# Decoder block on one core: FFN rows split before they are transposed, low parts of the GELU on GpSimd, scores at the head of a slot, and no zero products in the last stage

## The reference

```python
x = x + attn(layernorm(x), Wq, Wk, Wv, Wo, Wa, Wb, conv taps)   # gated delta rule, 16 heads of 128, values 256 wide
x = x + xattn(layernorm(x), ctx, ctx)                           # 32 query heads of 8 on 8 key/value heads
x = x + ffn(layernorm(x), w1, b1, w2, b2)                       # 256 -> 1024 -> 256

# xattn, per sequence and head, 64 x 64 scores
scores = q @ k.T / sqrt(8); attn = softmax(scores); out = attn @ v
# ffn
w1q, w2q = ternary(w1), ternary(w2)                # -1, 0, 1
h = gelu(x @ w1q.T + b1)                           # exact form
y = h @ w2q.T + b2
```

## Time and profile before

| | us |
|---|---|
| Median of three runs (2300.52 to 2302.37) | 2301.5 |
| Profiled execution, own time | 2296.62 |
| Its span | 2294.8 |
| Mean granted TensorE clock | 0.993 |
| PE busy | 2099.4 (91%) |
| DVE busy | 1846.1 (80%) |
| ACT busy | 1534.8 (67%) |
| POOL busy | 967.0 (42%) |

### The profile page before, as it was taken

One profiled execution on the slowest core, in us unless ns is written; L12 is line 12 of the kernel. 1 busy time (PEld: TensorE's weight loads), 2 busy tenths in 40 slices (PEclk: granted clock), 3 DMA queues, 4 the chain that ended last, 5 costly groups with the idle time before them and its releaser, 6 DMA issues.

```text
span 2294.8 us, 61471 instructions
## 1 busy us (share of the span) xinstructions
PE 2099.4 (91%) x23576; PEld 1356.7 (59%) x23576; DVE 1846.1 (80%) x2942; ACT 1534.8 (67%) x2881; POOL 967.0 (42%) x1312
## 2 busy tenths in 40 slices
PE   2499799999999999999999999999888889999998
PEld 2244365665665665665565665665555667777776
DVE  6888788898888889889888988889766556666665
ACT  3498677777777777777777777777656345555554
POOL 1006756282653827446283553827450112222222
PEclk9999999999999999999999999999999989999999
DMA  8535433333233333324323333332321200111100
GB/s 288 191 132 189 137 88 97 85 95 99 67 101 95 84 96 90 94 78 108 94 76 91 85 101 84 94 95 73 101 59 42 61 16 28 34 34 33 34 17 20
DMA packets 360817, 199.97 MB, mean 87 GB/s; under 512 B 304336, under 2 KB 313296, under 8 KB 358608
## 3 DMA queue, kind: packets, MB, share of 16 engines
q1 hardware_dynamic: 360528, 196.04, 30.2%
HBM read 123.87 MB, written 72.09 MB: 85 GB/s over the span
## 4 chain that ended last, share of the span: by engine, by line
PE 72%; ACT 12%; issue 6%; DVE 5%; POOL 3%; DMA 2%; SPq 1%; ACTq 0%; DVEq 0%; POOLq 0%
PE PS L1304 22%; PE PS L1318 15%; PE PS L1382 6%; PE PS L1397 5%; ACT XN L785 4%; PE PS L1553 4%; PE PS L1355 3%; ACT Y L762 3%; PE PS L1482 3%; PE PS L1515 3%; PE PS L1543 2%; PE PS L1339 2%; PE PS L1501 2%; PE PS L1346 2%; PE PS L1529 1%
## 5 line engine op out<-in xcount | busy, mean ns | idle before, releaser
L1031 DVE SCALAR_TENSOR_TENSOR Y<-PS,CW,Y 128x504 f32<-128x504 f32 (+2 forms) x1536 | 1114.3, 732 | 231.8 <-ACT Y L755 198.2
L1304 PE MATMUL PS<-XT,WH 128*128 128x512 f16 x2048 | 614.6, 382 | 6.6 <-DVE Y L1031 6.6
L755 ACT ACTIVATE Y<-PS,CW 128x512 f32<-128x512 f32 x512 | 394.3, 773 | 320.6 <-PE PS L1304 316.1
L1304 PE MATMUL PS<-XT,WL 128*128 128x512 f16 x1024 | 388.8, 380 | 0.0
L1318 PE MATMUL PS<-WOS,XN 128*128 128x256 f16 x3072 | 377.7, 273 | 3.4 <-DVE XN L1046 2.3
L1318 PEld LDWEIGHTS PS<-WOS,XN 128*128 128x128 f16 x3072 | 300.6, 98 | 94.0 <-DVE XN L1046 4.0
L610 POOL TENSOR_TENSOR SCR<-SCR 128x31 f32<-128x31 f32 (+15 forms) x496 | 288.5, 582 | 38.9
L1304 PEld LDWEIGHTS PS<-XT,WH 128*128 128x128 f16 x2048 | 168.5, 98 | 208.1 <-issue 40.5
L607 POOL TENSOR_TENSOR SCR<-SCR 128x31 f32<-128x31 f32 (+15 forms) x496 | 269.7, 544 | 38.9
L585 POOL TENSOR_SCALAR KD<-SCR 128x32 f32<-128x32 f32 x16 | 5.4, 339 | 659.9 <-DMA SCR<-PGD 659.9
L785 ACT ACTIVATE XN<-PS,KN 128x256 f32<-128x256 f32 x512 | 212.7, 466 | 14.3 <-PE PS L1318 14.3
(11 more groups left out here) (139 smaller groups left out, 2976.1 us busy)
## 6 DMA issues: line engine op xcount, KB each, us to landing
PGD<-SCR SPq DMA_DIRECT2D x128, 256.0 KB, 2.1
SCR<-PGD SPq DMA_DIRECT2D x128, 256.0 KB, 3.2
EQD<-XN SPq DMA_DIRECT2D x32, 512.0 KB, 2.6
SCR<-EQD SPq DMA_DIRECT2D x128, 128.0 KB, 2.6
SCR<-QND SPq DMA_DIRECT2D x128, 128.0 KB, 3.1
SCR<-in_wall SPq DMA_DIRECT2D x8, 1024.0 KB, 7.3
SCR<-PGD SPq DMA_DIRECT2D x64, 128.0 KB, 3.2
ED<-SCR SPq DMA_DIRECT2D x16, 512.0 KB, 2.8
```

The costliest lines, as they stand in the source:

```text
L755: A_.activation(Y[:, b, :], PJ[b][:, :], ACT.Identity, scale=CW[:, h[1] % NH, cw0 + 3:cw0 + 4], bias=CW[:, h[1] % NH, cw0 + 4:cw0 + 5]).th ...
L1031: V_.scalar_tensor_tensor(yv[:, :, m:T], pv[:, :, 0:T - m], CW[:, h[1] % NH, cw0 + 3 - m:cw0 + 4 - m], yv[:, :, m:T], ALU.mult, ALU.add).t ...
L1304: ins = mm(PJ[b][:, :], wt[:, c, w0:w0 + P], XT[:, g % 3, xi, :], start=(n == 0), stop=(n == 5))
```

## The change

It has four parts, all in the last stage.

1. `normalized_half` now also splits the rows: VectorE rounds the two normalized blocks to f16 and subtracts, into columns of XB that were unused. `half_transposed` transposes both f16 parts (eight f16 transposes, not four f32), into TRB[1] seen as f16. `ffn_rows` copies all four 256-column pieces at once (1024 elements a partition, not 512), and `hidden` and `transposes_of` wait for that copy. `low_rows` is gone. `normalized_half` moves from the end of slots 2 and 6 to between the two tiles of these slots.
2. `low_gelus` is gone from VectorE. GpSimd does it, piece by piece behind the rounding (`two_parts`). In GpSimd's order the two `rstd_half` now stand ahead of `two_parts`.
3. `scores` stands first in a slot, ahead of `weighted`.
4. The `keep_busy` calls inside the loop are gone, with their wait for `results`. Those ahead of the first scores stay.

```diff
-            def high_parts(i, hf):
+            def two_parts(i, hf):
                 n = 2 * i + hf
                 for f in range(4):
                     pool.wait_ge(S["gelu_done"], at(4 * n + f + 1))
                     pool.wait_ge(S["f2_mm"], at(max(n - 1, 0)))
                     nc.gpsimd.tensor_copy(HH[hf][:, f, :], H[hf][:, f, :]).then_inc(S["hh_done"], 1)
+                    pool.wait_ge(S["hh_done"], at(4 * n + f + 1))
+                    nc.gpsimd.tensor_tensor(HL[hf][:, f, :], H[hf][:, f, :], HH[hf][:, f, :], ALU.subtract).then_inc(S["hl_done"], 1)
...
                 if last:
-                    high_parts(i - 1, 0)
                     rstd_half(i - 1, 1)
+                    two_parts(i - 1, 0)
                 if following:
                     rstd_rows(i + 1)
                 if last:
                     biased(i - 1, 1)
-                    high_parts(i - 1, 1)
+                if live:
+                    rstd_half(i, 0)
+                if last:
+                    two_parts(i - 1, 1)
                 if following:
                     value_blocks(i + 1)
                 if live:
-                    rstd_half(i, 0)
                     biased(i, 0)
...
-                A_.activation(XB[:, hf, 0:2, 0:HT], TRB[1][:, :].rearrange("p (c t) -> p c t", c=2), ACT.Copy).then_inc(S["xh2"], 1)
+                A_.activation(XB[:, hf, :, 0:HT], TRH, ACT.Copy).then_inc(S["xh2"], 1)
...
+                dve.wait_ge(S["xl2"], at(n))
                 for p in (2 * hf, 2 * hf + 1):
                     V_.tensor_scalar(XN[:, 1, p, :], XC[i % 3][:, p, :], MV[:, 1, p, 0:1], RSTD[:, 1, p:p + 1],
                                     ALU.subtract, ALU.mult).then_inc(S["ln_b"], 1)
+                hi, lo = XB[:, hf, 0:2, HT:GT], XB[:, hf, 2:4, HT:GT]
+                rows = XN[:, 1, 2 * hf:2 * hf + 2, :]
+                dve.wait_ge(S["ln_b"], at(7 * n + 7))
+                V_.tensor_copy(hi, rows).then_inc(S["xhi"], 1)
+                dve.wait_ge(S["xhi"], at(n + 1))
+                V_.tensor_tensor(lo, rows, hi, ALU.subtract).then_inc(S["xl2"], 1)
...
             def half_transposed(i, hf):
-                pe.wait_ge(S["ln_b"], at(7 * (2 * i + hf) + 7))
-                for c in range(2):
-                    for a in range(2):
-                        ins = nc.tensor.transpose(TRB[1][:, HT * c + P * a:HT * c + P * a + P], XN[:, 1, 2 * hf + a, P * c:P * c + P], ident)
+                pe.wait_ge(S["xl2"], at(2 * i + hf + 1))
+                for k in range(2):
+                    for c in range(2):
+                        for a in range(2):
+                            ins = nc.tensor.transpose(TRH[:, 2 * k + c, P * a:P * a + P], XB[:, hf, 2 * k + a, HT + P * c:HT + P * c + P], IDH[:, :])
...
                 for u in range(8):
-                    fill = live and u not in (0, 4)
-                    if fill and u in (1, 5) and i:
-                        pe.wait_ge(S["x3_done"], at(2 * i - 2 + u // 4))
-                    if fill:
-                        keep_busy(5)
+                    if u < 6 and live:
+                        scores(i, u + 2)
+                    if u >= 6 and following:
+                        scores(i + 1, u - 6)
                     if u == 0 and last:
                         weighted(i - 1, 3)
                     if u in (2, 4, 6) and live:
                         weighted(i, u // 2 - 1)
-                    if fill:
-                        keep_busy(10 if u in (3, 7) else 4)
-                    if u < 6 and live:
-                        scores(i, u + 2)
-                    if u >= 6 and following:
-                        scores(i + 1, u - 6)
-                    if fill:
-                        keep_busy(12 if u in (1, 5) else 4)
                     if live:
                         transposes_of(i, u)
```

More of the change, by code:

```diff
@@ L193, in build @@
         HT = GT // 2
+        TRH = TRB[1][:, :].bitcast(F16).rearrange("p (k t) -> p k t", k=4)
         names = "ld_const ld_w0 ld_w1 ld_w2 ld_w3 ld_tern ld_tern2 w_split w_hi tern_sum tern_all tern_done zeroed conv_scaled idle_zero".split()
@@ L200, in build @@
                        st_pg0 st_pg1 st_qs0 st_qs1 ld_lp ld_bl ld_ql st_le ld_xa st_x1 ld_y0 ld_y1 ld_y2 ld_kg0 ld_kg1 ld_vt0 ld_vt1 st_out0 st_out1 st_out2""",
-            "pool": "rstd lane kg_zero vb_done rstd_a rstd_b hh_done b2_done",
+            "pool": "rstd lane kg_zero vb_done rstd_a rstd_b hh_done hl_done b2_done",
             "act": """xh_done gate_s dec_exp sq tap0 tap1 tap2 tap3 silu0 silu1 silu2 silu3 vw_ev n_ev qs_ev qt_done xh2 exp_done pt_done gelu_done""",
             "dve": """ln_step xl_done z_done gate_v rhq_done conv0 conv1 conv2 conv3 m_done vl_done pg_done xa_done
-                      kn_done ln_a ln_b xl2 mx_done sub_done rs_done ob_done nrm_done hl_done x3_done zero_e""",
+                      kn_done ln_a ln_b xhi xl2 mx_done sub_done rs_done ob_done nrm_done x3_done zero_e""",
             "pe": """tr_done gate_mm dec_mm proj0 proj1 proj2 proj3 vw_mm nu_mm qs_mm h_mm out_mm gr_mm
@@ L1185, in attended @@
                 V_.bn_stats(STT6[:, 1, p, :], XC[i % 3][:, p, :]).then_inc(S["ln_b"], 1)
[L1187 to L1197, removed]
             def results(i, hf):
@@ L1212, in _ @@
                         shifted_scores(i, u, 0)
[L1213 to L1216, removed]
+                    if u == 2 and last:
+                        normalized_half(i - 1, 1)
+                    if u == 6 and live:
+                        normalized_half(i, 0)
                     if live:
@@ L1223, in _ @@
                         moments(i - 1, 1)
-                    if u == 2 and last:
-                        normalized_half(i - 1, 1)
-                        low_gelus(i - 1, 0)
                     if u in (3, 5, 7) and live:
@@ L1236, in _ @@
                         moments(i, 0)
[L1237 to L1240, removed]
         @block.tensor
@@ L1496, in transposes_of @@
                     if j == 1 and u == 3 and i:
-                        pe.wait_ge(S["xl2"], at(2 * i))
+                        pe.wait_ge(S["xh2"], at(2 * i))
                     if j == 1 and u == 7:
-                        pe.wait_ge(S["xl2"], at(2 * i + 1))
+                        pe.wait_ge(S["xh2"], at(2 * i + 1))
                     for q in range(4):
@@ L1520, in hidden @@
                 n = 2 * i + hf
-                pe.wait_ge(S["xl2"], at(n + 1))
+                pe.wait_ge(S["xh2"], at(n + 1))
                 for f in range(4):
```

## The result

| | us |
|---|---|
| Before, median (2299.52 to 2303.06) | 2301.5 |
| Changed, median of 5 (2280.86 to 2288.86) | 2282.16 |
| Ratio changed to before, 95% interval | 0.9936 (0.9916 to 0.9956) |
| Changed, span of the profiled execution | 2280.3 |

The change makes the kernel faster by 19 us, less than 1%. I had forecast 55 us. The time lies inside the range; the gain is a third of what was forecast.

The account below looks back on a forecast made before the run. TensorE's own order, partly zero products, was taken to set the last stage's pace. Gains of 60.9 (halves) and 8 (iteration 0), less 1.4 (tail) and 12 (clock), made 55.5 us: 2246 us, range 2220 to 2294.

Parts of the forecast that it names:

- a): Half's start to slot 1's transposes: without zero products TensorE waits for ScalarE; gain 0.4 us, no more.
- b): Slot 1's transposes to half_transposed, 8.39 us: zeros go and scores first covers ScalarE's copy; gain 1.7 us.
- c): half_transposed to summed of slot 3, 5.68 us: VectorE's wait goes, ffn_rows' copy grows; gain 2.25 us.
- d): summed of slot 3 to the half's end, 8.88 us: no zero product stands here; gain 0.
- The other half loses the same: The group's other half, 29.65 us, has the same zeros and was to lose the same 4.35 us.
- a fall in six halves at 2 us: cost 12: Last stage's halves: clock falls where TensorE is light, in slot 1 waiting for ScalarE; cost 12 us (0 to 30).
- The bound of one half for each low us: Clock falls: 10.2 us at 0.50 loses at most 4.8 us, one of 3.4 us up to 1.7.
- I take 38: gain 8: Iteration 0, 46.20 us and held by VectorE, was to take 38 us; gain 8 (6 to 10).
- The tail: After the last group, 27.00 us: rounding and difference run one behind the other on GpSimd; cost 1.4 us (0 to 6).
- R1: Rival: transposes do not hold the clock, so falls in 14 halves cost 67 us; 2301, no change; chance 13%.
- R2: Rival: clock low through much of the last stage, slower; at 40% low 2322 us; chance 10%.
- R3: Rival: VectorE and GpSimd hold each other up, 1.2 us lost per half; 2263 us; chance 15%.

Follow-up runs that it names:

- best_a: zeros_in_waits with weighted ahead of scores in slot 6, 3 zeros there for 7, and 12 zeros in TensorE's first wait of iteration 0; 2241.0 us, ratio 0.9748.
- zeros_in_waits: The changed kernel with zero products put back only where TensorE waits for another engine anyway; 2243.2 us, ratio 0.9765 to before.
- best_b: best_a with 6 zeros in slots 2, 4 and 6 of iteration 0, where it had 4, none and 4; 2235.4 us, ratio 0.9716.

## Why the prediction was wrong, by its own steps

- **Steps a to d were right.** Per half: a) 5.17 to 4.84 us, gain 0.33 (0.4 forecast); b) 8.39 to 6.74, gain 1.65 (1.7); c) 5.68 to 3.25, gain 2.43 (2.25); d) 8.88 to 8.82. Sum 4.47 against 4.35. The eight f16 transposes, which no row had shown, took 0.61 us from first to last where the four f32 ones had taken 0.60.
- **"The other half loses the same" was off by 1 us.** It became 26.29, not 25.3. Scores first makes the next group's scores wait in slot 6 for the queries; `weighted`, which had stood there, covered that. I named what scores covers and not what `weighted` had covered. With `weighted` ahead of it there, and 3 zeros for 7, best_a took 25.77; the other half us I have not explained. With the last half (19.93 to 17.57 without a fall, 2.36 and not 4.35) it is 7 us in all.
- **The step that failed is the clock: "a fall in six halves at 2 us: cost 12".** Against the halves of zeros_in_waits (342.6, less 1.7 for the fall in its last one, so 340.9) the changed kernel lost 374.7 - 340.9 = 34 us, with 77 us low: 0.44 us lost per low us. The nine falls were 8.0 us long in the mean, some 3.5 us lost in each; the end of iteration 0's cost 2 more. The bound of one half for each low us was sound; I took the falls too short and too few. I looked at slot 1 and its like, slot 5, as one light place. Slot 5 is worse: its transposes are followed by a wait for their copy, the transposed rows, a wait for the queries, and scores and `weighted` of slot 6. Seven of the nine falls came from slot 5 to there and two in slot 1. Four of the seven began within that `weighted`, and the earlier trace rows had shown just this work ahead of a fall; in the forecast I used the row for slot 1 alone.
- **Iteration 0: "I take 38: gain 8", measured a loss of 4.3.** With the clock held it takes 39.5 (best_b), so the 38 was about right for the high clock. (I had cut it 2.6 us shorter, so it is 40.6 in this cut.) I had a sum for the low clock too, 40, with `weighted` at 2.05 where it takes 3.54 and without waits. I took 38, between it and VectorE's 36, and put nothing on the low clock, though the zeros were what kept the clock there.
- **The tail** cost 0.9 (1.4 forecast). GpSimd's difference took 1.20 (1.27), was hidden, and `ffn_rows` took 1.02 (1.03).
- **The terms together.** In the profiled executions the gain was 14.5 us, 41 less than the 55.5: 27 less in the halves (22 by the clock, 7 by the other half, less 2.4 for a fall that the kernel before had itself), 12 in iteration 0, 3 ahead of the stage, and half a us the other way in the tail.
- **Rivals.** R1's 67 us was too high by 33 where my 12 was too low by 22, and the f32 transposes of zeros held the clock, against its cause. R2 is what the old order does without zeros. R3's contention is there and has no price.

With the clock all but kept in the halves the time was 2243.2 (zeros_in_waits). That it is near the 2246 is luck: the 2246 had 12 us for falls in it, and without any the prediction had 2234. The range held the time of 2282 only because it allowed for R1, whose mechanism the run speaks against.

Left open: what exactly decides whether a light place falls. Places with the same work fell in some iterations and not in others, and with TensorE busy for 1.5 us of the stretch ahead as well as for 2.6.

## What to carry to other kernels

Before taking filler work out of TensorE's queue, mark for each filler what it stands in: on the path it costs its time, in a wait it costs nothing and may be what holds the clock. Take out the first kind only. Where an order is changed, price what each moved step had covered for others, not only what it will cover.

## What was not expected of the hardware

- The small f32 products of `weighted` (64 columns of weights, 18 moving) take 1.98 us per 64 at 1.00 and 3.54 at 0.50, 1.8 times as long.
- 0.44 us was lost for each us at the low clock (33.8 of 76.7), in halves where TensorE is busy for 84% of the time.
- VectorE's instructions with SBUF operands took 0.70 for 0.41 (normalized rows) and 1.27 in the mean, 0.69 at best (difference, line 1169), beside GpSimd's differences. GpSimd's own took 1.15 to 1.48.
- 106 f32 transposes of zeros left the clock of iteration 0 as 106 products with zeros did: 0.93 and 0.92, against 0.50 with neither.
